# Routing arithmetic, row normalisation and two projections reordered ahead of the expert stage of a fused attention and expert kernel

## What is computed

```
xn  = (x - mean) / sqrt(var + eps)            # x: 8 batches x 512 rows x 128
q, k, v = xn @ Wq + bq, xn @ Wk + bk, xn @ Wv + bv     # 8 heads of 16
attn = softmax(q k^T / 4);  out = attn v1 - lam * attn v2
s   = (0.2 * (layernorm(out) * ln_w + ln_b)) @ Wo + bo
h   = mod(int(xn[:, 0] + xn[:, 1]), 8)        # the expert of a row; the second is h + 1
g   = silu(mean over both experts of relu(xn @ W1[e] + b1[e]) @ W2[e] + b2[e])
y   = x + s * g
```

## Time and profile before

| | us |
|---|---|
| median of 3 runs | 409.66 |
| lowest and highest | 409.14, 410.87 |
| the profiled execution, its own time | 411.52 |
| its span, first to last instruction | 409.6 |
| PE busy in the span | 381.5 (93%) |
| DVE, ACT, POOL busy | 291.8, 267.5, 189.3 |

### The profile page before, as it was taken

How to read it: one execution, slowest core, us unless ns; L and a number is a source line. 1 busy time by engine, 2 the same in 40 slices (tenths; PEclk the granted TensorE clock), 3 DMA queues, 4 the chain that set the end, 5 groups by cost and what they waited for, 6 DMA issues and landing times.

```text
span 409.6 us, 8427 instructions
## 1 busy us (share of the span) xinstructions
PE 381.5 (93%) x2576; PEld 248.3 (61%) x2576; DVE 291.8 (71%) x758; ACT 267.5 (65%) x667; POOL 189.3 (46%) x262
## 2 busy tenths in 40 slices
PE   4996989999999999999999999999999999999993
PEld 2353876565775667766665668765676667764321
DVE  7787996656686757766676767866686767866884
ACT  3581756666765776576666767676766668675783
POOL 7944203454456543565355532663573444541200
PEclk9996999999999999999999999999999999999999
DMA  7975953263216451265105640346136141216740
GB/s 263 343 230 112 242 196 91 80 206 105 79 37 191 111 195 21 79 190 168 46 27 170 189 140 18 136 121 197 48 127 216 22 169 47 81 26 213 230 159 26
DMA packets 36945, 54.75 MB, mean 134 GB/s; under 512 B 6724, under 2 KB 25141, under 8 KB 36903
## 3 DMA queue, kind: packets, MB, share of 16 engines
q1 hardware_dynamic: 31456, 46.94, 34.6%
q0 software_dynamic: 3296, 6.76, 7.8%
q10 hardware_dynamic: 2151, 0.53, 0.6%
HBM read 15.59 MB, written 6.75 MB: 55 GB/s over the span
## 4 chain that ended last, share of the span: by engine, by line
PE 74%; DVE 7%; DMA 5%; ACT 4%; SPq 4%; issue 4%; POOL 1%; ACTq 0%; DVEq 0%; POOLq 0%
PE ring L1393 14%; PE pv_bank L1327 13%; PE ring L1414 12%; PE score L1289 12%; PE exp L1314 10%; PE ring L1251 3%; DVE neg_max L1049 3%; DMA xs<-xn_rows,inverse 3%; SPq L532 2%; PE ring L1335 2%; PE ring L1255 1%; PE ring L1353 1%; PE ring L1276 1%; PE ring L1375 1%; PE score L1264 1%
## 5 line engine op out<-in xcount | busy, mean ns | idle before, releaser
L1049 DVE TENSOR_REDUCE neg_max<-score 128x1 f32<-128x512 f32 x256 | 169.0, 683 | 72.3 <-PE score L1289 66.7
L1289 PE MATMUL score<-ks,qs 96*128 96x512 bf16 x256 | 98.3, 386 | 6.3 <-DVE neg_max L1049 6.0
L787 ACT ACTIVATE probs<-exp 128x512 f32<-128x512 f32 x124 | 72.5, 605 | 36.3 <-PE exp L1314 32.3
L787 ACT ACTIVATE xin<-exp 128x512 f32<-128x512 f32 x120 | 69.7, 604 | 38.5 <-PE exp L1314 38.1
L1314 PE MATMUL exp<-qs,ks 99*128 99x512 bf16 x244 | 91.7, 380 | 0.1
L825 ACT ACTIVATE hT<-ring,pair 128x128 f32<-128x128 f32 x256 | 73.4, 377 | 13.0 <-PE ring L1393 11.9
L1414 PEld LDWEIGHTS ring<-w_sb,hT 128*128 128x128 f32 x568 | 73.5, 191 | 10.4 <-issue 3.5
L1414 PE MATMUL ring<-w_sb,hT 128*128 (+1 forms) x568 | 75.4, 275 | 0.9 <-ACT hT L825 0.9
L1393 PEld LDWEIGHTS ring<-xsT,pair 128*128 128x128 f32 x512 | 66.3, 191 | 14.6 <-issue 8.1
L1393 PE MATMUL ring<-xsT,pair 128*128 128x128 f32 x512 | 68.2, 276 | 1.7 <-issue 1.2
L684 POOL TENSOR_SCALAR tanh<-tanh 128x128 f32<-128x128 f32 x32 | 17.2, 536 | 95.5 <-ACT tanh L845 95.2
(11 more groups left out here) (198 smaller groups left out, 417.4 us busy)
## 6 DMA issues: line engine op xcount, KB each, us to landing
pair<-table SPq DMA_DIRECT2D x32, 580.0 KB
qs<-parts SPq DMA_DIRECT2D x42, 128.0 KB
ks<-parts SPq DMA_DIRECT2D x42, 128.0 KB
xin<-_attn_hidden_states_dram SPq DMA_DIRECT2D x8, 256.0 KB, 4.4
table<-in_L_ffn_W_dram SPq DMA_DIRECT2D x2, 1024.0 KB, 9.2
w_sb<-in_L_ffn_W_dram SPq DMA_DIRECT2D x8, 256.0 KB, 10.4
xn_rows<-xn SPq DMA_DIRECT2D x8, 256.0 KB, 3.0
table<-_attn_hidden_states_dram SPq DMA_DIRECT2D x8, 256.0 KB, 5.4
```

What stands on the lines that cost most here:

```text
L787: a.activation(prob(n), exp_banks[n][:, :], ACT.Exp, scale=SCALE).then_inc(exp_done, 1)
L1049: v.tensor_reduce(neg_max[:, b % 2, col:col + 1], score_bank[n % 2][:, :], AX.X, ALU.max, negate=True).then_inc(max_taken, 1)
L1289: t.matmul(score_bank[n % 2][:, :], qs[0:MAX_ROW, b % STK, hh, c * P:(c + 1) * P], ks[0:MAX_ROW, b % STK, hh, :], start=True, stop=True).t ...
```

## The change

- `LN_GROUPS` ends in (4,6), (6,7), (7,8); for batches 4 to 7 POOL now makes `shift` at once behind the last power operation. Batch 4 is normalised by ACT, between the eviction of peel 0 0 2 and that of peel 0 1 2; batch 2 already behind batch 1, batch 3 ahead of project 1 0.
- The sum of two columns has twice the mean taken off before `rstd` is there, so L1019 and L892 go. Three conversions of type (L897, L901, L903) go, `h` being kept in whole numbers. The running sum is written one place on, so that it excludes its own row and the subtraction L911 goes.
- The second half of the token table (L948) is made by ACT, behind a new semaphore `in_tile_ready`, between project 1 1 and peel 1 0 1.
- "route 1" stands ahead of peel 0 1 2 and transpose_x 1 on PE. Peel 1 0 2 stands behind score 1, peel 1 1 2 behind score 5; their evictions on ACT stand behind load_small.
- SP stores batch 2 ahead of batch 0's parts, and sends part 2 of k (stack_part 0 1 2) behind batches 4, 5 and 6 and ahead of 7 and 3. "ones" moves from ACT's queue to SP's, ahead of load_w2.
- In the extra tiles turn_tile stands a little further ahead of hidden and most down steps one score later. From tile 7 on PE's and POOL's order stays as it was; for 11 tiles from 11 to 38 "tanh" stands behind one more step of ACT (ten times an exponential).

```diff
-LN_GROUPS = ((0, 1), (1, 2), (2, 4), (4, 6), (6, 8))
-POOL_NORM = (4, 5, 6, 7)
+LN_GROUPS = ((0, 1), (1, 2), (2, 4), (4, 6), (6, 7), (7, 8))
+POOL_NORM = (5, 6, 7)
+LATE_SHIFT = 4
-SHIFT_AT = (-58.5, -57.5, -55.5, -53.5, -50)
-NORM_AT = (-58, -56.4, -49.9, -47.93, -49.2, -49.1, -49, -48.95)
+SHIFT_AT = (-58.5, -57.5, -55.5, -53.5, -53.4, -50)
+NORM_AT = (-58, -56.4, -56.3, -48.61, -48.7, -48.68, -48.66, -48.63)
-PEEL_AT = (((-55.5, -55.3), (-55.4, -55.25)), ((-45.5, -45.3), (-45.4, -45.2)))
+PEEL_AT = (((-55.5, -55.3), (-55.4, -48.65)), ((-45.5, 1.5), (-45.4, 5.3)))
...
-TOKENS_AT = -45
+TOKENS_AT = -45.6
-EXTRAS_AT = 5.2
-GROUPS_AT = (9.05, 10.72, 13.05, 14.05)
+EXTRAS_AT = 5.9
+GROUPS_AT = (9.05, 10.72, 12.55, 14.05)
-FFN_FIRST = 7.6
+FFN_FIRST = 8.6
-TX, DX = 2.4, 3.2
+TX, DX = 3, 3.2
-INIT_AHEAD = 1.5
+INIT_AHEAD = 1.67
-SPLIT_MAX, TURN_MAX = 16.8, 18.9
+SPLIT_MAX, TURN_MAX = 16.5, 18.9
-TANH, GATE = 0.7, 1.84
+TANH, GATE = 1, 1.84
...
-                    if end < B:
+                    if first < LATE_SHIFT:
                         g.tensor_scalar(shift[:, tok], mv[:, tok, 0], -1.0, None, ALU.mult)
...
+                    if end == B:
+                        late = slice(C * LATE_SHIFT, NT)
+                        pool.wait_ge(rstd_ready, len(LN_GROUPS))
+                        link(g.tensor_scalar(shift[:, late], mv[:, late, 0], -1.0, None, ALU.mult))
+                        g.tensor_tensor(shift[:, late], shift[:, late], rstd[:, late], ALU.mult).then_inc(shift_ready, 1)
...
+                elif kind == "tokens":
+                    act.wait_ge(in_tile_ready, 1)
+                    a.activation(token[:, 1, :, :, :], in_tile, ACT.Copy, scale=row_of[:, 0:1]).then_inc(token_ready, 1)
...
-                link(v.tensor_copy(n_abs[:, :], whole_i))
-                link(v.tensor_tensor(over, n_abs[:, :], v_abs[:, :], ALU.is_gt))
-                link(v.tensor_tensor(n_abs[:, :], n_abs[:, :], over, ALU.subtract))
-                link(v.scalar_tensor_tensor(h[:, :], sign[:, :], -1.0, n_abs[:, :], ALU.add, ALU.mult))
-                link(v.tensor_copy(whole_i, h[:, :]))
-                link(v.tensor_scalar(whole_i, whole_i, EXP - 1, None, ALU.bitwise_and))
-                link(v.tensor_copy(h[:, :], whole_i))
+                link(v.tensor_tensor(over, whole_i, v_abs[:, :], ALU.is_gt))
+                link(v.tensor_tensor(n_abs[:, :], whole_i, over, ALU.subtract))
+                link(v.scalar_tensor_tensor(h_i[:, :], sign[:, :], -1.0, n_abs[:, :], ALU.add, ALU.mult))
+                link(v.tensor_scalar(h_i[:, :], h_i[:, :], EXP - 1, None, ALU.bitwise_and))
...
-                link(v.tensor_tensor_scan(flat, work[:, 512:768], zeros,
-                                          0.0, ALU.add, ALU.add))
-                v.tensor_tensor(seen[:, :, :], seen[:, :, :], onehot[:, :, :], ALU.subtract).then_inc(seen_ready, 1)
+                v.tensor_tensor_scan(work[:, 768:1024], work[:, 511:767], zeros,
+                                     0.0, ALU.add, ALU.add).then_inc(seen_ready, 1)
...
-                v.tensor_scalar(token[:, 1, :, :, :], in_tile, row_of[:, 0:1], None, ALU.mult).then_inc(token_ready, 1)
```

More of the change, by code:

```diff
@@ L429, in gated_attention_moe @@
         token_ready = sem("token_ready")
+        in_tile_ready = sem("in_tile_ready")
         slots_split = sem("slots_split")
@@ L533, in _ @@
                                          parts_of(b)[:, i, k, :]).then_inc(stacked[b % STK], 16)
+                elif kind == "ones":
+                    sp.wait_ge(dve_consts, 1)
+                    for slot_b in range(STK):
+                        sp.dma_start(ks[MAX_ROW:KROWS, slot_b, :, :],
+                                     ones_bf[:, :].unsqueeze(1).to_broadcast([PARTS, HEADS, S])).then_inc(ones_stacked, 16)
                 elif kind == "load_w2":
@@ L632, in _ @@
                                     ALU.pow).then_inc(rstd_ready, 1)
-                    if end < B:
+                    if first < LATE_SHIFT:
                         pool.wait_ge(rstd_ready, s[1] + 1)
                         g.tensor_tensor(shift[:, tok], shift[:, tok], rstd[:, tok], ALU.mult).then_inc(shift_ready, 1)
+                    if end == B:
[3 more added lines that the diff above has]
+                        g.tensor_tensor(shift[:, late], shift[:, late], rstd[:, late], ALU.mult).then_inc(shift_ready, 1)
+                        pool.wait_ge(shift_ready, EARLY_GROUPS + 1)
                 elif kind == "norm" and s[1] in POOL_NORM:
                     b = s[1]
-                    pool.wait_ge(shift_ready, 1 + [b >= end for _, end in LN_GROUPS].index(False))
                     for t in range(C * b, C * b + C):
@@ L727, in _ @@
                     act.dma_start(lnb_sb[:, :], ln_b.rearrange("(p a) -> p a", a=1)).then_inc(small_loaded, 16)
-                elif kind == "ones":
-                    act.wait_ge(dve_consts, 1)
-                    for slot_b in range(STK):
-                        act.dma_start(ks[MAX_ROW:KROWS, slot_b, :, :],
-                                     ones_bf[:, :].unsqueeze(1).to_broadcast([PARTS, HEADS, S])).then_inc(ones_stacked, 16)
                 elif kind == "copy_ninth":
@@ L860, in _ @@
             v.memset(zeros, 0.0)
+            v.memset(work[:, 767:768], 0.0)
             link(v.memset(va[:, :, :, :, HD:VW], 0.0))
@@ L889, in count_groups @@
                 dve.wait_ge(pair_summed, 1)
+                dve.wait_ge(rstd_ready, len(LN_GROUPS))
                 link(v.tensor_tensor(v01[:, :], v01[:, :], rstd[:, :], ALU.mult))
-                dve.wait_ge(shift_ready, len(LN_GROUPS))
-                link(v.scalar_tensor_tensor(v01[:, :], shift[:, :], 2.0, v01[:, :], ALU.mult, ALU.add))
                 link(v.scalar_tensor_tensor(v_abs[:, :], v01[:, :], -1.0, v01[:, :], ALU.mult, ALU.max))
@@ L945, in find_tokens @@
                 dve.wait_ge(slots_split, 1)
-                link(v.tensor_tensor(in_tile, by_pair(slot_tile[:, 0:NT], FT), over_pairs(columns[:, :, :], NT // 2), ALU.is_equal))
-                v.tensor_tensor(token[:, 0, :, :, :], in_tile, by_pair(ordinal[:, :], FT), ALU.mult)
-                v.tensor_scalar(token[:, 1, :, :, :], in_tile, row_of[:, 0:1], None, ALU.mult).then_inc(token_ready, 1)
+                v.tensor_tensor(in_tile, by_pair(slot_tile[:, 0:NT], FT), over_pairs(columns[:, :, :], NT // 2),
+                                ALU.is_equal).then_inc(in_tile_ready, 1)
+                dve.wait_ge(in_tile_ready, 1)
+                v.tensor_tensor(token[:, 0, :, :, :], in_tile, by_pair(ordinal[:, :], FT), ALU.mult).then_inc(token_ready, 1)
             def find_rows(q):
@@ L1014, in _ @@
                         continue
-                    tok = slice(C * first, C * end)
-                    v.tensor_tensor(v01[:, :], xin[:, :, 0], xin[:, :, 1], ALU.add).then_inc(pair_summed, 1)
-                    dve.wait_ge(rstd_ready, g + 1)
+                    link(v.tensor_tensor(v01[:, :], xin[:, :, 0], xin[:, :, 1], ALU.add))
                     dve.wait_ge(stats_ready, end)
-                    v.scalar_tensor_tensor(shift[:, tok], mv[:, tok, 0], -1.0, rstd[:, tok],
-                                           ALU.mult, ALU.mult).then_inc(shift_ready, 1)
+                    v.scalar_tensor_tensor(v01[:, :], mv[:, :, 0], -2.0, v01[:, :],
+                                           ALU.mult, ALU.add).then_inc(pair_summed, 1)
                 elif kind == "transpose_x" and s[1] not in PEELED:
```

16 lines of the change are left out of this document (8 added, 8 removed).

## The result

The changed kernel takes 409.22 us (median of 12 runs, 407.06 to 409.97), the kernel before 410.77 in the runs beside it (12 runs, 409.14 to 411.57). The ratio is 0.9957, 95% interval 0.994 to 0.9974: a gain of 1.6 to 1.8 us, where 3.4 was forecast.

A forecast was written before the change was run, and what follows sets the result against it. PE's own work bounds the long stage, so time can be won only ahead of about 41 us. Gather 2.2 earlier plus clock 1.2 gave 3.4 us: 409.66 to 406.3, range 404.8 to 408.6 (8 in 10).

The forecast's parts named there:

- Parts 1 to 4: Head: last power operation ends 17.0, count starts 19.3, DVE goes on 1.24 earlier at 20.4, last row table 27.97.
- Part 5: PE up to the inversion: inversion ends at 28.4 against 30.60, first gather starts at 29.2, 2.2 earlier.
- Part 6: Eight stores ahead of the first gather: last lands by 28.3, 0.9 before 29.2; cost 0, up to 1.
- Part 7: From first gather to tile: gather takes 4.89 again (4.2 to 5.7), data at 34.1; xsT at 34.9, 2.4 earlier.
- Rival B: ACT's queue ahead of xsT of tile 0 becomes the bound: gather's gain 1.2, time 408.1; chance 0.14.
- Part 8: Peels in PE's wait for the first gather keep the clock at 2.4 GHz: gain 1.2 (0.4 to 2.2).
- part 9: Long stage: PE's and POOL's orders unchanged from tile 7, later tanh have room; 0, bounds 0.4 either way.
- Rival A: Clock falls all the same in PE's wait for the first gather; only 2.2 left, 407.5; chance 0.17.
- Rival C: Long stage: eleven later tanh find no room and reach PE, 6.6 less 3.4: slower, 412.9; chance 0.06.

The follow-up runs named there:

- before_same: The kernel before, unedited, run and profiled once more; ratio 1.0 to the kernel before.
- before_fill: The kernel before with 12 unread matmuls in PE's pauses behind scores 1 to 5; ratio 0.9942.
- peels_only: The kernel before with only the two second peels of batch 1 moved behind the inversion (behind scores 1 and 5); ratio 0.9966 to the kernel before.
- before_new_extras: The kernel before with only the changed kernel's new order of the extra tiles; ratio 1.0012 to the kernel before.
- after_peels_ahead: The changed kernel with the two second peels of batch 1 put back ahead of the inversion; ratio 1.0027 to the kernel before.
- after: The changed kernel as made, in its first runs and first profile; 409.22 us, ratio 0.9957 to the kernel before.
- after_same: The changed kernel, unedited, run and profiled once more; ratio 0.9968 to the kernel before.
- after_down6: The changed kernel with the last extra tile's down step put one score earlier; ratio 0.9956 to the kernel before.
- old_extras_again: Repetition of after_old_extras: the changed kernel with the extra tiles in the old order; ratio 0.993 to the kernel before.
- after_small_later: The changed kernel with the ten small loads issued later on ACT's queue, four behind the second tile's eviction, six behind the fourth's; ratio 0.9963.
- head_only: The changed kernel with the old order of the extra tiles and the second peels of batch 1 ahead of the inversion; ratio 1.0035 to the kernel before.
- old_extras_fills: The changed kernel with the old order of the extra tiles, four unread matmuls behind peel 1 1 2 and five behind exp 8; ratio 0.9958.
- after_fill: The changed kernel with 8 unread matmuls behind score 3, score 4 and peel 1 1 2; ratio 0.9962 to the kernel before.
- after_gather8_early: The changed kernel with POOL gathering tile 8 ahead of the first load_y_init; ratio 0.9933 to the kernel before.
- after_small_tiny: The changed kernel with the ten small loads cut to one partition, values that depend on them left wrong; ratio 0.993 to the kernel before.
- old_extras_gather8: The changed kernel with the old order of the extra tiles and tile 8 gathered ahead of the first load_y_init; ratio 0.9935.
- after_old_extras: The changed kernel with the extra tiles put back where the kernel before has them; ratio 0.9922 to the kernel before.
- after_fill_late: The changed kernel with six unread matmuls behind exp 8, in PE's later pause; ratio 0.9945 to the kernel before.

## Why the prediction was half right

One table holds the case. Times of the profiled executions, from the timelines; clock by the stretches.

| kernel | inverse ends | second tile | first y_sb | first pv | span | clock low, PE at work |
|---|---|---|---|---|---|---|
| before_same | 31.66 | 38.17 | 65.98 | 72.61 | 409.5 | 35 to 42, 403 to 406 |
| before_fill | 30.93 | 37.06 | 63.74 | 70.34 | 406.1 | 401 to 403 |
| peels_only | 30.82 | 36.56 | 63.21 | 69.83 | 405.6 | never |
| before_new_extras | 32.07 | 38.75 | 66.48 | 73.10 | 408.9 | 35 to 42, 403 to 406 |
| after_peels_ahead | 31.61 | 38.86 | 67.36 | 75.24 | 411.3 | 35 to 42, 72 to 76 |
| after (first profile) | 28.98 | 35.65 | 62.77 | 69.36 | 405.3 | never |
| after_same | 29.75 | 36.35 | 63.77 | 71.63 | 407.8 | 69 to 73 |
| after_down6 | 29.05 | 35.72 | 62.39 | 70.17 | 406.4 | 67 to 71 |
| old_extras_again | 29.03 | 35.65 | 62.30 | 68.94 | 405.9 | never |
| after_small_later | 28.99 | 34.40 | 63.46 | 70.08 | 406.5 | 400 to 403 |

**Parts 1 to 4** hold, each within 0.3 us. Integer operands cost what float ones cost (0.18).

**Part 5** holds. It said 2.2 between the two inversions; the ends of `inverse` show 31.15 - 28.98 = 2.2 in the first pair of profiles and 31.66 - 29.75 = 1.9 in the second. head_only shows its reason too: with the peels in front, PE's arrival and not DVE's tables sets the time.

**Part 6** was wrong about the stores, at a small price: it put them at nothing, with 0.9 to spare. In after the last store is issued at 25.46 and lands 3.3 later (DMA view of its issue), at 28.8, where 28.3 was forecast:

```profile
xn_rows<-xn SPq DMA_DIRECT2D x1, 256.0 KB, 3.3
```

POOL then starts at 29.66, 0.88 behind that landing and 0.68 behind `inverse`; before_same has 0.3 behind `inverse`. In twelve profiles `inverse` ends by 29.8. In ten of them the gather starts 0.88 or 0.89 behind the landing of the last store, in the other two (after_same, old_extras_fills) 0.3 behind `inverse`. So in those ten the stores set the start: they cost 0.4 in after and from 0.2 to 1.1 over the ten. What the 0.88 consists of is not shown. The dearest case is after_small_later, where the profile itself puts the wait down to the last store:

```profile
30.40 1.22 POOL L664 DMA_INDIRECT xs<-xn_rows,inverse  x1 [6.66 <-DMA xn_rows<-xn]
```

**Part 7.** Its gather of 4.89, with bounds of 4.2 to 5.7, took 5.13 and 4.04 in the two profiles, and the second 4.73 in after_same. Its upper bound was too low: after_fill's took 7.58. Rival B did not happen: in after ACT's queue was in time, and in after_same xsT of tile 0 came directly behind the peels' evictions, at 35.30, 0.5 behind its product, but the second tile had to wait until 36.35 for its gather. The second tile came 1.8 earlier.

**Part 8, the clock, first half.** Right, and by its reason: in every profile with peels in the gap the clock is at 2.4 GHz there, but for after_fill, whose gather came latest and kept PE idle for 2.32. From the second tile to the first y_sb the kernel before takes 27.8 at the low clock and 26.7 without it (before_fill). That is 1.1, where 1.2 was forecast.

**The step that failed** is the other half of part 8 and part 9: the new order of the extra tiles was taken at nothing ("DVE ... has the same work in another order (down steps one score later)"), and the stretch around the first y_sb was passed over ("PE's and POOL's orders are unchanged from tile 7 on"). Two things happen there.
- From the second tile to the first y_sb, at full clock, the old order takes 26.6 or 26.7 (old_extras_again, peels_only), the new one 27.1 and 27.4 (after, after_same). That is 0.5 to 0.8. With the last down step alone put back it is 26.7 (after_down6).
- From the first y_sb to the first pv the profiles of the table with the clock up take 6.6, and those with it down 7.8 or 7.9 (after_same, after_down6, after_peels_ahead): 1.2. Of the nine profiles with the new order and no late fillers five fell there, of the eight with the old order none. Where it fell, PE had waited 1.12 to 1.72 for tile 8 and 0.4 more for DVE just behind (or, in after_gather8_early, 2.61 for DVE); with the old order the wait for tile 8 is 0.57 to 0.73. The length of the wait does not decide alone: after_small_tiny waited 1.20 and 0.43 for the same two, and old_extras_gather8 1.50 for DVE, and the clock stayed up in both.

The line of after_small_tiny and that of old_extras_gather8 (timelines of PE):

```profile
66.21 0.33 PE L1382 MATMUL ring<-ident,xs 128*128 128x128 f32 x1 [1.20 <-DMA xs<-xn_rows,inverse]
```

```profile
67.43 0.39 PE L1294 MATMUL score<-ks,qs 96*128 96x512 bf16 x1 [1.50 <-DVE neg_max L1054]
```

The mean clock of the timed executions agrees only in part. It is 0.997 or more in 3 of 24 of the changed kernel (after and after_same together), in 2 of 12 of after_down6, in 7 of 12 of after_gather8_early, in 8 of 9 with the late fillers, and in 11 of 12 of after_old_extras and its repetition; but only in 5 of 12 of old_extras_gather8 and 6 of 12 of old_extras_fills, which have the old order too. It can't say where the clock fell: after_small_later's mean is 0.993 in the profiled execution, from a fall in the last microseconds of PE's work alone. The median span is 407.4 for after_same, 405.6 for the late fillers, 405.4 for after_old_extras and 405.0 for old_extras_again.

So the sum is 1.8 + 1.1 - 0.7 - 1.2 = 1.0 up to the first pv in the profiled pair. The long stage adds 0.7 (336.9 against 336.2 from the first pv to the end), which makes 1.7, as the two spans have it: 409.5 - 407.8. The 0.7 is more than the 0.4 that part 9 allowed, but it is no mark of the change. In before_same the clock fell a second time, while PE still had work to do at the end (PE by stretches):

```profile
403.00:404.00 1.00, 0.74 (x5) 0.73 0.00 0
404.00:405.00 1.00, 1.00 (x6) 0.50 0.00 0
```

From the start of its last product with v to the end of PE's work that execution takes 10.0, and after_same, whose clock is up there, 9.1. The first profile of the kernel before has no such fall (9.0), so it comes and goes with the execution. The pair's 1.7 therefore holds 0.9 that one execution of the kernel before lost at its end, and the ratios of many executions (1.3 to 1.8 us) are the better measure.

**Rival A** gave nearly the right time (407.5 where 407.9 was measured on that footing) by the wrong place: the clock fell, but 30 us later than it says, and behind another pause. The two parts that it shares with the forecast, a gather 2 us earlier and PE idle a while, were real. Rival B's 408.1 is nearer still, and that is luck: its mechanism cost nothing. **Rival C** did not happen. POOL's waits for the store of a tile (the waits between 75 and 370 us, first before_same, then after_same) are as frequent in both kernels, which the one profile of the earlier trace rows had not shown:

```profile
POOL y_sb L678 <- DMA y_rows<-y_sb,inverse: 8.5, 17, 1.7
```

```profile
POOL y_sb L691 <- DMA y_rows<-y_sb,inverse: 10.0, 17, 2.3
```

**What is shown and what is open.** Shown by runs: the price of the low clock in the kernel before (before_fill), the worth of the peels and that they and the short head pay only together (peels_only, head_only, after_old_extras), that the new order costs 1.5 us behind the changed head (after_old_extras and its repetition) and that gathering tile 8 early wins most of the same, the packets' part in the gathers (after_small_later). Shown in profiles, and supported by a gain of 0.7 us whose interval overlaps that of the changed kernel: the second fall of the clock (after_fill_late). Argued: that this fall and the 0.5 to 0.8 make up the 1.5. Open: what besides the length of the wait decides whether the clock falls; where it fell in the executions of peels_only (8 of 11), old_extras_gather8 and old_extras_fills that have a mean under 0.997 (their profiles show no fall while PE works); why head_only is slower than the kernel before; and which constants of the order, besides the last down step, carry the loss.

The version to keep is after_old_extras: 0.9922 and 0.993, against 0.9957 and 0.9968 for the change as made.

## What to carry to other kernels

A change that brings work forward also moves every later pause. After pricing the place it aims at, look in PE's timeline for the next stretch in which PE is short of work (here PE's wait of 0.57 at 69.8 us in the kernel before) and ask whether the change makes that pause longer: a wait grown from 0.57 to 1.72 us came with a fall of the clock that cost 1.2 us, though waits of 1.20 and 1.50 did not always bring one. Look at several executions, since one profile of each kernel (the first pair here) shows no second fall at all; and move work in front of a pause, or behind it, before adding any. A DMA issue on ACT's queue cost it about 0.5 us (six took 3.1 in after_small_later, ten 5.5 in after; loads of one partition took 0.27 each), so such issues belong where the engine would idle. And a wait for several things has a runner-up: here the last store stood close behind `inverse`, and took its place in ten of twelve profiles as soon as `inverse` came earlier.

## What the runs showed of the hardware

- Matmuls that nobody reads are worth 2.4 us net in a gap at 34 to 37 us (before_fill), and 0.7 at 67 to 70 us (after_fill_late against the mean of the changed kernel's two ratios; the intervals overlap).
- The gather's start stands 0.88 or 0.89 us behind the landing of the last store in the ten profiles in which the store came last, and 0.3 behind DVE's `inverse` where that came last.
- The second indirect gather of 128 rows of 512 bytes landed at most 2.8 us after its issue beside 20 packets of queue 10 or none (2.42, at most 2.5, at most 2.8 in three kernels), and after 3.88 to 6.66 beside the packets of the small loads (4.73 beside 1267 in after_same). The slowest gather of all in that stretch took 7.58.
- A power operation on POOL took 1.67 us for 8 columns and 1.04 for 4, so cutting a group in two costs 0.41 more in all.
- PE's first products are slow at a clock that the profile gives as 1.00. The groups of instructions of PE in after, from 10 to 14 us (busy, mean ns of one):

```profile
L1256 PE MATMUL ring<-xT,wqk 128*128 128x512 f32 x3 | 2.9, 1105 | 0.8 <-ACT xT L758 0.8
```

The same form takes less than half of that later (four in 1.98 us at 22.76). What slows it was not tried.
